# A graph-attention and mixture-of-experts kernel: a chunk's finishing and routing move from stops between loops into the items of one quad, and source columns are loaded ahead of destination rows

## The reference, cut to what matters

```python
def _L0_gnn_ref(x, src, dst, Wq, bq, Wk, bk):     # x comes in normalised
    q = jnp.tanh(x @ Wq + bq)                     # 25 columns
    k = x @ Wk + bk
    w = jnp.sum(q[s] * k[d], axis=1) / d_k        # s, d: edges and self loops
    wmax = jax.ops.segment_max(w, d, num_segments=N)
    ew = jnp.exp(w - wmax[d])
    alpha = ew / denom[d]                         # denom: segment sum of ew
    out = jax.ops.segment_sum(alpha[:, None] * x[s], d, num_segments=N)
...
x = x + _L0_gnn_ref(_layernorm(x), src, dst, ...)
x = x + _L0_ffn_ref(_layernorm(x)[None], ...)[0]  # 8 experts, each row goes to its top 2
```

## Time and profile before

| | |
|---|---|
| median of 3 runs | 1678.6 us (1676.88 to 1678.79) |
| profiled execution | 1678.56 us, span 1676.8 us |
| POOL busy | 1101.1 us (66%) |
| PE matmul busy | 1124.2 us (67%) |
| DVE busy | 827.7 us (49%) |
| ACT busy | 519.4 us (31%) |
| granted TensorE clock, mean | 0.749 of full speed |

### The profile page before, as it was taken

One profiled execution on the slowest core, in us unless ns is written; L12 is line 12 of the kernel. 1 busy time (PEld: TensorE's weight loads), 2 busy tenths in 40 slices (PEclk: granted clock), 3 DMA queues, 4 the chain that ended last, 5 costly groups with the idle time before them and its releaser, 6 DMA issues.

```text
span 1676.8 us, 30544 instructions
## 1 busy us (share of the span) xinstructions
PE 1124.2 (67%) x6718; PEld 767.1 (46%) x6719; DVE 827.7 (49%) x3273; ACT 519.4 (31%) x1474; POOL 1101.1 (66%) x1099
## 2 busy tenths in 40 slices
PE   5935655655665665556565656555647999999997
PEld 5922332423342333234232423232335888888886
DVE  7724444565466545655664565457553232322322
ACT  2522222322232323233232213222322333434332
POOL 2047777767776777677677766777703667766675
PEclk9997656666566756666676566666767999999999
DMA  9475444555456445555544564456442454544543
GB/s 200 98 170 131 129 127 128 148 145 131 129 143 159 131 127 146 150 134 143 155 130 127 141 163 113 128 147 163 124 135 44 92 98 67 99 96 94 98 69 63
DMA packets 155748, 210.05 MB, mean 125 GB/s; under 512 B 59525, under 2 KB 122589, under 8 KB 155558
## 3 DMA queue, kind: packets, MB, share of 16 engines
q0 software_dynamic: 61360, 151.84, 37.4%
q1 hardware_dynamic: 73217, 38.82, 9.7%
q10 hardware_dynamic: 21110, 18.79, 4.4%
HBM read 174.49 MB, written 34.41 MB: 125 GB/s over the span
## 4 chain that ended last, share of the span: by engine, by line
PE 38%; POOL 21%; issue 16%; DVE 11%; DMA 7%; DVEq 4%; ACT 3%; ACTq 1%; POOLq 0%; SPq 0%
POOL arena_a L539 20%; PE pb L1595 9%; PE pb L1587 8%; PE pb L1466 6%; DMA arena_a<-rows_dram,idx 3%; PE pb L1519 2%; PE pb L1390 2%; DVEq L314 2%; DMA arena_b<-xn_dram,gidx 2%; PE pb L1451 2%; DMA out_dram<-arena_b,tokB 2%; PE pb L1513 2%; PE pb L1442 2%; PE pb L1572 1%; PE pb L1543 1%
## 5 line engine op out<-in xcount | busy, mean ns | idle before, releaser
L539 POOL DMA_INDIRECT arena_a<-rows_dram,idx x848 | 814.3, 960 | 380.7 <-issue 257.1
L1466 PE MATMUL pb<-arena_a,arena_b 128*64 128x257 f32 x1696 | 329.9, 557 | 12.8 <-ACT arena_b L1255 12.8
L1442 PE MATMUL pb<-ident,qs 128*128 128x128 f32 x212 | 64.1, 398 | 289.5 <-ACT qs L1240 262.7
L879 DVE SCALAR_TENSOR_TENSOR acc<-acc,alpha,pb 32x257 f32 x424 | 203.3, 480 | 77.3 <-issue 67.6
L1466 PEld LDWEIGHTS pb<-arena_a,arena_b 128*64 128x64 f32 x1696 | 159.9, 196 | 142.7 <-issue 112.1
L597 POOL DMA_INDIRECT out_dram<-arena_b,tokB x104 | 166.3, 1599 | 86.0 <-DVE arena_b L1121 65.7
L1587 PE MATMUL pb<-arena_b 128*128 128x256 f32 x832 | 190.5, 383 | 1.2 <-ACT arena_b L1345 1.2
L1595 PE MATMUL pb<-arena_b 128*128 128x256 f32 x832 | 188.2, 379 | 0.0
L861 DVE CUSTOM_DVE_ANT_0 arena_b<-pb,mask,nmo 128x512 f32<-128x512 f32 x106 | 79.6, 751 | 212.5 <-PE pb L1451 203.7
L1442 PEld LDWEIGHTS pb<-ident,qs 128*128 128x128 f32 x212 | 27.5, 182 | 323.4 <-ACT qs L1240 294.1
L1587 PEld LDWEIGHTS pb<-arena_b 128*128 128x128 f32 x832 | 159.7, 192 | 23.7 <-ACT arena_b L1345 1.6
(11 more groups left out here) (221 smaller groups left out, 1264.5 us busy)
## 6 DMA issues: line engine op xcount, KB each, us to landing
arena_a<-rows_dram,idx POOLq DMA_INDIRECT x848
arena_b<-dst_dram SPq DMA_DIRECT2D x212, 64.0 KB
arena_b<-in_L_ffn_W_dram SPq DMA_DIRECT2D x16, 512.0 KB, 5.0
rows_dram<-acc SPq DMA_DIRECT2D x14, 493.5 KB, 6.0
xn_dram<-arena_a ACTq DMA_DIRECT2D x7, 910.0 KB, 8.7
acc<-in_x_dram SPq DMA_DIRECT2D x13, 448.0 KB, 13.9
out_dram<-arena_a ACTq DMA_DIRECT2D x13, 448.0 KB
idx<-srccol SPq DMA_DIRECT2D x214, 2.0 KB
```

The lines of the kernel that those rows point to most:

```text
L539: g.indirect_dma_start(out=xg[:, (s * 2 + x_) * G + j, :], out_offset=None, in_=rows_dram[:, :], in_offset=bass.IndirectOffsetOnAxis(ap=id ...
L879: ins = v.scalar_tensor_tensor(out=mine, in0=mine, scalar=alpha[rows_of, b:b + 1], in1=sums_bank[b][rows_of, 0:W1COLS], op0=ALU.mult, op1= ...
L1442: last = nc.tensor.transpose(pb[0][:, x_ * P:(x_ + 1) * P], qs[:, x_, :, :].rearrange("p j s -> p (j s)"), ident[:, :])
L1466: last = mm(sums_bank[b][HP * x_:HP * x_ + HP, 0:W1COLS], probT[:, b, j * P + HP * x_:j * P + HP * x_ + HP], xg[:, (s * 2 + x_) * G + j, 0 ...
```

## The change

A chunk's `finished` and `route` are now called from inside the one quad that stood between the two stops; the loops over the other quads keep the plain body. In that quad (items a = 2 to 5 of the quad's own counting, j = 0 to 3):

- DVE: `finished` behind `add_sums` in j = 0; the bias of the logits (`logits_of`) behind the maximum in j = 1; `route` behind `add_sums` in j = 2. Inside `finished` the first four tiles are normalised before the statistics of the last three.
- ACT: `finished` between `copy_qT` and `exponentials` in j = 1, `store_x2` behind that item; `route` and the loads of the next chunk's x between `copy_qT` and `exponentials` in j = 3. The second inverse deviation now comes behind the copies of the first four tiles.
- PE: `finished` between `sums` and `prob_transposes` in j = 1, `route` in the same place in j = 3. `last_sums` and `fresh_quad` go. The results of these products move to PSUM banks 0, 1 and 2.
- The first quad that may hold a chunk's finishing can be one earlier, since the sums of one more item are in by then (`chend` + 1 in place of + 2).
- SP: for each slot it waits for the gathers of item a and loads the sources of item a+4, then waits for the mask of item a-2 and loads the destinations of item a+2. Every load that was issued still is; the destinations of the last item come behind the loop.

```diff
@@ SP @@
-                    sp.wait_ge(s_mask, number(s + 1))
-                    sp.sem_inc(tk_s, 1)
-                    load_targets(sp, s, group, s + XSLOTS)
                     sp.wait_ge(s_g[s], sp.to_reg(k * (32 * G) + 32 * G))
                     sp.sem_inc(tk_s, 1)
                     load_sources(sp, s, group, s + XSLOTS)
+                    sp.wait_ge(s_mask, number(s + 1))
+                    sp.sem_inc(tk_s, 1)
+                    load_targets(sp, (s + PEEL) % XSLOTS, group, s + PEEL)
@@ DVE, prologue @@
+            v.sem_inc(s_mask, PEEL)
@@ DVE @@
-            def quad(k):
+            def quad(k, c=None):
                 for j in range(4):
                     a = PEEL + j
                     maximum(a % 2, tiles, a, number)
+                    if c is not None and j == 1:
+                        logits_of(c)
                     edge_mask(...)
                     add_sums((a - 1) % 2, tiles, a - 1, number(a + XSLOTS), number(a + 1))
+                    if c is not None and j == 0:
+                        v.wait_ge(s_acc, number(a + 2))
+                        v.sem_inc(tk_v, 1)
+                        finished(c)
+                    if c is not None and j == 2:
+                        route(c)
...
+                residual(parts[0])
+                statistics(parts[0])
+                residual(parts[1])
+                v.wait_ge(a_rw, (c + 1) * 16)
+                v.sem_inc(tk_v, 1)
+                normalise(0, parts[0])
+                statistics(parts[1])
+                normalise(1, parts[1])
...
-                v.wait_ge(s_acc, v.to_reg(hi * 4 + 3))
-                v.sem_inc(tk_v, 1)
-                finished(c)
                 with v.Fori(hi, hi + 1) as k:
-                    quad(k)
-                route(c)
+                    quad(k, c)
@@ ACT @@
                 copy_q(a_ % XSLOTS, landed)
                 copy_qT(number(a_ + 1))
+                if between is not None:
+                    between()
                 exponentials(a_ % 2, number(a_ + 1))
...
+                between = {} if c is None else {1: lambda: finished(c), 3: rows_out}
...
+                    if c is not None and j == 1:
+                        store_x2(c)
@@ ACT, finished @@
-                for u in range(CH):
-                    a.wait_ge(a_tp, c * CH + u + 1)
...
+                    for u in range(lo_, hi_):
+                        a.wait_ge(a_tp, c * CH + u + 1)
@@ PE @@
                 if not first:
                     sums((a - 1) % 2, (a - 1) % XSLOTS, number(a), number(a))
+                if between is not None:
+                    between()
                 prob_transposes(a % 2, number(a + 1))
...
+                between = {} if c is None else {1: lambda: finished(c), 3: lambda: route(c)}
...
-                hi = segment_quads(c)
-                last_sums(PEEL + 3, counter(pe, pe.snap(hi - 1)))
-                finished(c)
-                fresh_quad(hi)
-                last_sums(PEEL + 3, counter(pe, hi))
-                route(c)
+                lo, hi = segment(pe, c)
+                with pe.Fori(lo, hi) as k:
+                    quad(k)
+                with pe.Fori(hi, hi + 1) as k:
+                    quad(k, c)
```

More of the change, by code:

```diff
@@ L1255, in copy_probs, with item @@
                 nc.scalar.copy(probT[:, b, :], pb[2][:, :]).then_inc(s_pts, 1)
-            def item(tiles, a_, number, landed):
+            def item(tiles, a_, number, landed, between=None):
                 copy_q(a_ % XSLOTS, landed)
                 copy_qT(number(a_ + 1))
+                if between is not None:
+                    between()
                 exponentials(a_ % 2, number(a_ + 1))
@@ L1267, in _, with quad, rows_out @@
                 item(tiles, i, number, 32 * G)
-            def quad(k):
+            def quad(k, c=None):
+                def rows_out():
+                    route(c)
+                    next_rows(c)
+                between = {} if c is None else {1: lambda: finished(c), 3: rows_out}
                 number = counter(a, k)
@@ L1271, in quad @@
                 for j in range(4):
-                    item(tiles, PEEL + j, number, a.to_reg(k * (32 * G) + 32 * G * ((PEEL + j) // XSLOTS + 1)))
+                    item(tiles, PEEL + j, number, a.to_reg(k * (32 * G) + 32 * G * ((PEEL + j) // XSLOTS + 1)), between.get(j))
+                    if c is not None and j == 1:
+                        store_x2(c)
             def load_x(c):
@@ L1469, in sums, with item @@
                 last.then_inc(s_pv, 1)
-            def item(a, number, first=False):
+            def item(a, number, first=False, between=None):
                 q_transposes(number(a + 1))
@@ L1484, in _, with quad @@
             number = counter(pe, 0)
-            def quad(k, fresh=False):
+            item(0, number, first=True)
+            item(1, number)
+            def quad(k, c=None):
+                between = {} if c is None else {1: lambda: finished(c), 3: lambda: route(c)}
                 number = counter(pe, k)
                 for j in range(4):
-                    item(PEEL + j, number, first=fresh and j == 0)
-            def last_sums(a, number):
-                sums(a % 2, a % XSLOTS, number(a + 1), number(a + 1))
-            def fresh_quad(lo):
-                with pe.Fori(lo, lo + 1) as k:
-                    quad(k, fresh=True)
-            def segment_quads(c):
-                lo, hi = segment(pe, c)
-                fresh_quad(lo)
-                with pe.Fori(lo + 1, hi) as k:
-                    quad(k)
-                return hi
-            item(0, number, first=True)
-            item(1, number)
-            last_sums(1, number)
+                    item(PEEL + j, number, between=between.get(j))
             def transposes_a(c, u):
@@ L1535, in route @@
                 pe.wait_ge(a_as, c + 1)
[L1536 removed]
+                at = pb[0][:, D:D + width]
+                mm(at, tri[:, :], flat, start=True, stop=False, skip_group_check=True)
                 for d in range(1, CH + 1):
[L1538 removed]
+                    last = mm(at[:, d * NE:width], ones_b[:, :], flat[:, 0:width - d * NE],
                               start=False, stop=d == CH, skip_group_check=True)
```

55 lines of the change are left out of this document (27 added, 28 removed).

## The result

The changed kernel takes 1667.1 us (median of 4 runs, 1665.3 to 1670.1); the kernel before, beside it, 1678.5 (4 runs, 1676.9 to 1678.8). The ratio is 0.9945, 95% interval [0.9928, 0.9962]: 0.55% faster. I had said 1688, range 1669 to 1702, and gave faster a chance of 0.25.

What follows compares the result with a forecast made beforehand. GpSimd's gathers were taken to set the edge stage's pace, with 37.4 us of real stalls. 1678.6 + 11.5 (six chunks, 1.9 us more each) - 1.6 (last chunk) = 1688.5, stated as 1688, range 1669 to 1702.

Steps and rivals of the forecast that it cites:

- S(66): Start of TensorE's `q_transposes` of item 66, the next quad's first, in the fourth chunk; forecast at 61.4 us.
- step 1: Finishing inside the merged quad: the third item's transposes were to start 28.9 us after the first's.
- step 2: The one item between finishing and routing, at catch-up pace: 7.57 us, its successor starting at 36.5.
- step 4: Work behind routing, item 65's exponential to the next quad, with ScalarE's uncovered 3.18 us loop turn: 5.6 us lead gone.
- G(69): GpSimd's first gather of item 69 in the fourth chunk, due at 58.6 us; forecast start 67.9, stalled 9.3.
- What bounds the kernel: Edge stage: GpSimd's gathers set the pace; at most 37.4 us of real stalls in six chunks could be taken away.
- S(64): Start of TensorE's `q_transposes` of item 64, third of the finishing quad; forecast 28.9 us behind the first item's.
- Steps 3 and 4: Routing, ending at 53.3 us, 5.6 ahead of before, then the work and ScalarE's turn behind it, until 61.4.
- Step 5: GpSimd's late gather: one stall of 9.3 us in place of 7.4, the next hidden behind it; 1.9 us more per chunk.
- SyncE's loads at nothing: SyncE's new load order: same loads issued, slack falling from 18 to some 8 us, costed at nothing.
- The tail: Last chunk's finishing: first normalised tile 1.6 us sooner, and all behind it moving along.
- The turns shrink: Rival: cheaper loop turns on ScalarE (3.2 us off) and VectorE (5.3 off) give 1669 us; chance 0.25.

Runs made afterwards that it cites:

- f1: The kernel before, stops kept, with the change's new inner order of finishing on VectorE and ScalarE: 1665.3 us, ratio 0.9945.
- e4: The changed kernel with finishing's old inner order: 1679.0 us, ratio 1.0031 to the kernel before.
- g5: The changed kernel with 24 small copies at the end of ScalarE's loop over chunks: 1672.0 us, ratio 0.9982 to the kernel before.
- h2: The changed kernel with finishing's old inner order and 24 small copies at the end of ScalarE's loop over chunks: 1682.2 us, ratio 1.0040.
- e1: The kernel before with SyncE's part of the change alone: 1676.6 us, ratio 1.0015.
- e2: The changed kernel with SyncE's part undone: 1668.9 us, ratio 0.9968 to the kernel before.
- e3: The changed kernel with routing's pieces moved into the quad after the one with finishing's: 1656.3 us, ratio 0.9885 to the kernel before.
- f5: The changed kernel with ScalarE's loop over chunks laid at another place of its instruction memory: 1666.1 us, ratio 0.9947 to the kernel before.
- g1: The changed kernel with nine small copies at the end of ScalarE's loop over chunks: 1668.5 us, ratio 0.9956 to the kernel before.
- f2: The changed kernel with branch hints on the loops over chunks of VectorE, ScalarE and TensorE: 1666.3 us, ratio 0.9955 to the kernel before.
- f3: e3 with branch hints on the loops over chunks of VectorE, ScalarE and TensorE: 1642.4 us, ratio 0.9817 to the kernel before.
- f4: The kernel before with branch hints on the loops over chunks of VectorE, ScalarE and TensorE: 1668.4 us, ratio 0.9966.
- g2: f1 with branch hints on the loops over chunks of VectorE, ScalarE and TensorE: 1658.4 us, ratio 0.9899 to the kernel before.
- g4: The changed kernel itself, run on a slow chip where the kernel before took 2131.5 us: 2031.1 us, ratio 0.9545.

## Why the prediction was wrong

Three terms of the sum were too long, and together they put S(66) 3.6 us too late: finishing in step 1 (1.25 us), the item between in step 2 (0.55) and, the largest, ScalarE's turn in step 4, taken as 3.18 us and measured at 1.29. The stall before G(69) is shorter by the same 3.7 us. Beside that, the base was too high, and the gain of finishing's inner order was not in the sum.

- **What bounds the kernel**: right. Taken away from the time between the first and the last gather, stalls and pauses leave 1069.4 to 1072.8 us in each of the fourteen profiles in the tables. But I carried the fourth chunk's 7.4 us to six chunks, 44.4, where all stalls of before are 37.4 by the prediction's own first paragraph, 6.2 a chunk.
- **Step 1, finishing**: S(64) is 27.7 after S(62) in the mean of six chunks, not 28.9. Of the 1.25 us, 0.5 is item 63, which starts at 9.7 in place of 10.2; 0.4 is the chain from first transposes to the end of the bias, 8.8 us and not 9.15; the rest lies around the two. "The new order of the two inverse deviations costs nothing" is wrong: VectorE waits 1.57 us for the second one in the fourth chunk of the changed kernel, 2.25 in f1. And I never asked what the early normalising gives. The step has TensorE wait for `sums` of item 62 alone, as if the old order's tile were hidden under them; e4 shows that it isn't (16.5 for the first transposes, not 15.8). Net of its cost the order takes 1.0 us out of finishing with stops and 1.1 merged, and that is 0.55% (f1) to 0.86% (e4) of the time. In my text it gained 1.6 us once, in the last chunk.
- **Step 2, one item between**: 7.0 and not 7.57 us, 34.7 in place of 36.5 together with step 1.
- **Steps 3 and 4, routing and the turn**: from S(65) to S(66) 23.1 and not 24.9 us. ScalarE's turn is the term that was mis-sized: I took 3.18 us from before, where it follows a store at the end of routing, for a turn that follows a copy; it is 1.29. With ScalarE held for 1.7 us more (g5) the median is 6.4 us higher (0.40%), with the old order (h2 beside e4) 0.09%. Routing's own length was right: it ends 17.0 us behind S(65), where I had 16.8.
- **Step 5, GpSimd's slot**: the place is right (G(69), once a chunk), and the second stall hides behind the first, but for 0.7 to 0.8 us in two chunks. The stall follows S(66) one for one: S(66) 3.6 us earlier than forecast, mean stall 5.6 in place of 9.3.
- **SyncE's loads at nothing**: right as far as the intervals tell (e1, e2).
- **The tail**: 0.9 to 1.5 us in place of 1.6, but not by the step: the last chunk's first transposes start 1.55 us sooner behind the first operation of finishing (5.39 in place of 6.94), and the bias only 0.57 (15.30 in place of 15.87). "All behind it moves along" is wrong, again by the wait for the second inverse deviation. The rest is within what the tail varies by: e1's is 2.9 us longer than that of the kernel before, with the same work in it.
- **Rivals**: "The turns shrink" came out, with its figure of 1669, but that is luck in part: its reason covers only ScalarE's turn; VectorE's was 5.06, and the stalls fell by 2.0 us in all, not by the 7.8 of that rival. No rival named the inner order, without which the change loses. That merging makes the kernel slower holds for the old order only, and for at most 0.31% (e4).

What stays open: why ScalarE's turn is 1.3 us in the changed kernel and about 4 in e3 with the same pieces. e3's loop over chunks holds the code of three quads in place of two; that its length makes the turn dear was not tested. Open, too, is what makes GpSimd's pauses: the programs with stops have four (6.1 to 6.2 us), the changed kernel, e2, e4, f5 and g1 two (3.0 to 3.1), e3, f2, f3, g5 and h2 none. So some 3 us of the changed kernel's gain come from there and not from any step of mine.

## What to carry to other kernels

When a change has two edits in one function, cost the small one by itself, for its gain too: here a reordering of four calls on VectorE, with ScalarE's copies to match, carried all of a gain that a large restructuring was made for, and doing it alone (f1) was enough. Follow each engine that the reordering touches to the end of the piece: of the 1.8 us that the first transposes won in f1, 0.8 were lost again by the bias. Look for who waits for the first tile of a batch, and give it out before the second half is begun. A stall that once lay under a longer one can be priced only on the new path: a loop's turn measured behind one instruction is not a price for the same turn behind another.

## What the runs showed of the hardware

- The turn of the loop over chunks took ScalarE 1.27 to 1.31 us in the changed kernel and its near variants, 1.41 to 1.44 with a hint (f2, f3) and 3.85 to 4.42 in e3 without; VectorE 4.3 to 5.8 (2.2 to 2.6 with a hint, 2.95 in f4 and g2); and TensorE 4.5 to 4.7 in the kernel before, 4.6 with the hint (f4). Behind a store, in the kernel before, ScalarE's was 3.18.
- Nine three-column copies took 0.95 us on ScalarE and 24 took 2.36, about 0.1 us each; ahead of a turn of 1.29 us the nine delayed the next copy by 0.2.
- GpSimd makes single pauses of 1.7 to 1.9 us at the second gather of an item, always of the same ones: 26, 38, 86 and 98 in the kernel before, 26 and 86 in the changed one, none in e3, f2, f3, g5 and h2, and every twelfth item from 14 to 98 on the slow chip (g4). No cause shows in the trace.
- On the slow chip, GpSimd was busy for 1103.0 us (1101.2 in the changed kernel's first profile) and the tail took 466.1 (459.6), but from the first gather to the last went 1465.5 us in place of 1110.3. The waits of g4:

```profile
POOL arena_a L541 <- issue: 242.3, 746, 3.0
POOL arena_a L541 <- remote: 238.9, 88, 3.1
POOL arena_a L541 <- PE pb L1496: 169.3, 13, 13.7
```

88 pauses of 2.7 us, each before the first gather of an item, have no releaser in the trace, and the stalls for `sums`, 13 of them in place of 6, are 13 us each, twice the usual. There the changed kernel gains 4.5% in place of 0.55%. No trace of the kernel before was taken there, so where its 100 us went stays open. The record gives this chip the number of the one that ran e1 to e4 and took 1674.2 us for the kernel before; unless the number stands for two chips, the slowness came and went.
